# A dynamic depthwise convolution whose taps are three half-precision products instead of one f32 product

## What is computed

```python
def _L1_conv_ref(x, w1, b1, w2, b2):          # x is normalised over channels
    pooled = x.mean(axis=(2, 3))
    h = gelu(pooled @ w1.T + b1)               # exact gelu
    wdyn = (h @ w2.T + b2).reshape(Bs, Cs, 9)  # nine taps for every image and channel
    xp = pad(x, 1, mode='reflect')
    for i in range(3):
        for j in range(3):
            out += xp[:, :, i:i+32, j:j+32] * wdyn[:, :, 3*i+j, None, None]
```

## Time and profile before

| | us |
|---|---|
| median of three runs | 2282.22 |
| lowest, highest | 2279.48, 2284.02 |
| the profiled execution's span | 2530.8 |
| TensorE busy in that span | 1850.5 |
| VectorE busy | 1499.0 |
| ScalarE busy | 1020.8 |
| GpSimd busy | 1003.1 |

### The profile page before, as it was taken

The page is one execution under the profiler, slowest core; times in us unless marked ns, Lnnn a source line. Parts: engine busy times, 40 slices in busy tenths (PEclk is TensorE's granted clock), DMA queues, the critical chain, the costliest instruction groups (busy, mean ns, idle before and its releaser), DMA issues.

```text
span 2530.8 us, 39768 instructions
## 1 busy us (share of the span) xinstructions
PE 1850.5 (73%) x8630; PEld 970.6 (38%) x8631; DVE 1499.0 (59%) x5297; ACT 1020.8 (40%) x1718; POOL 1003.1 (40%) x1180
## 2 busy tenths in 40 slices
PE   0487776777767754999999994988888856888823
PEld 0343332333333322444444442554554433444412
DVE  2766554555545543777677773555555545777768
ACT  0433232332323322666666663434333323555411
POOL 0002344333443343665565564133333323665510
PEclk9788888788887876999999997988888867999955
DMA  9200101001010013222222222111111003222134
GB/s 269 78 17 26 35 33 34 27 26 34 32 34 28 18 39 79 70 67 68 69 65 69 67 69 59 56 51 50 50 51 50 16 16 87 67 68 65 46 116 149
DMA packets 180056, 148.97 MB, mean 59 GB/s; under 512 B 19302, under 2 KB 161822, under 8 KB 179960
## 3 DMA queue, kind: packets, MB, share of 16 engines
q1 hardware_dynamic: 153336, 98.05, 13.8%
q0 software_dynamic: 26624, 49.93, 5.6%
HBM read 76.00 MB, written 77.34 MB: 61 GB/s over the span
## 4 chain that ended last, share of the span: by engine, by line
PE 29%; issue 26%; DVE 16%; another core or an unknown queue 12%; ACT 7%; SPq 5%; DMA 3%; POOL 2%; ACTq 1%; DVEq 0%; POOLq 0%
PE banks L892 7%; PE banks L694 5%; PE banks L695 5%; PE banks L696 5%; PE banks L689 3%; ACT work L980 3%; PE banks L707 3%; SPq L478 2%; SPq L407 1%; DVE small L1282 1%; DMA work<-slot_rows 1%; SPq L479 1%; POOL ffn_rows L609 1%; DVE small L1167 1%
## 5 line engine op out<-in xcount | busy, mean ns | idle before, releaser
L609 POOL DMA_INDIRECT ffn_rows<-work x448 | 469.4, 1048 | 354.2 <-issue 201.8
L588 POOL DMA_INDIRECT slot_rows<-work,small x384 | 387.2, 1008 | 543.8 <-DVE small L1454 422.1
L689 PE MATMUL banks<-small,work 128*128 128x128 f32 x1920 | 301.2, 295 | 276.5 <-ACT work L980 87.9
L689 PEld LDWEIGHTS banks<-small,work 128*128 128x128 f32 x1920 | 242.5, 152 | 385.1 <-issue 187.5
L892 PE MATMUL banks<-work 128*128 128x512 f32 x576 | 301.3, 671 | 0.9 <-DVE work L1716 0.9
L694 PE MATMUL banks<-work,wb_h 128*128 128x512 f16 x648 | 247.2, 382 | 29.9 <-issue 17.7
L1660 DVE TENSOR_TENSOR work<-work 128x512 f16<-128x512 f32 x376 | 259.0, 689 | 12.6
L695 PE MATMUL banks<-work,wb_h 128*128 128x512 f16 x648 | 245.8, 379 | 0.0
L696 PE MATMUL banks<-work,wb_l 128*128 128x512 f16 x648 | 245.8, 379 | 0.0
L694 PE MATMUL banks<-work,wa_h 128*128 128x512 f16 x576 | 241.0, 418 | 3.5 <-ACT work L1011 3.2
L695 PE MATMUL banks<-work,wa_h 128*128 128x512 f16 x576 | 241.4, 419 | 0.0
(11 more groups left out here) (243 smaller groups left out, 2987.7 us busy)
## 6 DMA issues: line engine op xcount, KB each, us to landing
work<-slot_rows SPq DMA_DIRECT2D x112, 264.0 KB
work<-ffn_rows SPq DMA_DIRECT2D x48, 512.0 KB, 4.2
ffn_rows<-small SPq DMA_DIRECT2D x32, 256.0 KB, 3.8
work<-in_x SPq DMA_DIRECT2D x16, 512.0 KB, 3.3
out_image<-work SPq DMA_DIRECT2D x16, 512.0 KB, 2.6
ffn_rows<-work POOLq DMA_INDIRECT x448
slot_rows<-work,small POOLq DMA_INDIRECT x384
slot_rows<-small SPq DMA_DIRECT2D x17, 264.0 KB, 4.0
```

The lines of the kernel that those rows point to most:

```text
L588: pool_e.indirect_dma_start(slots, bass.IndirectOffsetOnAxis(ap=slot_i[:, row_buffer(p, i, k), tt:tt + 1], axis=0), rows[row_buffer(p, i, ...
L609: pool_e.indirect_dma_start(dst, bass.IndirectOffsetOnAxis(ap=idg[old.v][:, qq, 0:1].bitcast(I32), axis=0), yt[old.u][:, qq, :], None, bou ...
L689: last = pe.transpose(dst[:, tt * P:(tt + 1) * P], x, ident)
```

## The change

The tap values and the image are each split into a high and a low part in half precision (f16). A tap is then high x high, high x low and low x high: three f16 matmuls for each half, summed in PSUM. `vpad` has two planes, its inside is filled with the high part by ScalarE, and VectorE subtracts it from the f32 value in PSUM for the low part (semaphore `C_low`), for which GpSimd's border copies and the transposes of the rows now wait instead of `C_inside`. The border copies take both planes at once. On VectorE `split_taps` scales the nine values by a power of two (largest magnitude, exponent bits, its inverse) and splits them in six instructions; the diagonals take both parts in one instruction per third, of 768 elements in f16 instead of 384 in f32. ScalarE's copy of the result to `cacc` multiplies by the power of two. Before the first image one copy makes an f16 identity.

```diff
@@ scratch
-        wd = t([TAPS])
+        wd = t([TAPS + 1])
+        wd_exp, wd_down = t([1]), t([1])
+        wd_up = t([2, 1])
+        wd_hl = t([2, TAPS], F16)
-        vpad = [tC([HP, WP]) for _ in range(2)]
-        diag = tC([TAPS, P])
+        vpad = [tC([2, HP, WP], F16) for _ in range(2)]
+        diag = tC([2, TAPS, P], F16)
+        ident16 = tC([P], F16)
@@ GpSimd, c_step
-                    pool_e.wait_ge(sem("C_inside"), nxt.b + 1)
+                    pool_e.wait_ge(sem("C_low"), nxt.b + 1)
-                    pool_e.tensor_copy(v[:, 0:1, 1:W + 1], v[:, 2:3, 1:W + 1]).then_inc(sem("C_border_done"), 1)
+                    pool_e.tensor_copy(v[:, :, 0, 1:W + 1], v[:, :, 2, 1:W + 1]).then_inc(sem("C_border_done"), 1)
...
@@ TensorE, tap
-                for half in range(2):
-                    h0 = half * (H // 2)
-                    last = pe.matmul(pair[i.u][:, half * 512:(half + 1) * 512], diag[:, k, :],
-                                     vpad[i.u][:, h0 + dy:h0 + dy + H // 2, dx:dx + W],
-                                     start=(k == 0), stop=(k == TAPS - 1))
+                for w, v in ((0, 0), (0, 1), (1, 0)):
+                    for half in range(2):
+                        h0 = half * (H // 2)
+                        last = pe.matmul(pair[i.u][:, half * 512:(half + 1) * 512], diag[:, w, k, :],
+                                         vpad[i.u][:, v, h0 + dy:h0 + dy + H // 2, dx:dx + W],
+                                         start=(k == 0 and w + v == 0), stop=(k == TAPS - 1 and w == 1))
@@ TensorE, c_step
-                    pe.wait_ge(sem("C_inside"), upto(old.b + 3, IMAGES))
+                    pe.wait_ge(sem("C_low"), upto(old.b + 3, IMAGES))
                     route_turn("C_", old)
@@ ScalarE, c_step
-                    act.activation(vpad[nxt.u][:, 1:H + 1, 1:W + 1], tp.rearrange("p (h w) -> p h w", h=H), ACT.Copy,
+                    act.activation(vpad[nxt.u][:, 0, 1:H + 1, 1:W + 1], tp.rearrange("p (h w) -> p h w", h=H), ACT.Copy,
-                    act.activation(cacc, pair[i.u], ACT.Copy).then_inc(sem("C_conv_copied"), 1)
+                    act.activation(cacc, pair[i.u], ACT.Copy, scale=wd_up[:, i.u, :]).then_inc(sem("C_conv_copied"), 1)
@@ VectorE
+            def split_taps(i):
+                ...
+                dve.tensor_reduce(wd_exp, wd, AX_X, ALU.max, apply_absolute_value=True).then_inc(sem("dve_steps"), 1)
+                step()
+                dve.tensor_scalar(wd_exp.bitcast(I32), wd_exp.bitcast(I32), 0x7F800000, None, ALU.bitwise_and).then_inc(sem("dve_steps"), 1)
+                step()
+                dve.tensor_scalar(down.bitcast(I32), wd_exp.bitcast(I32), -1.0, float(0x7E800000), ALU.mult, ALU.add).then_inc(sem("dve_steps"), 1)
+                step()
+                if some(i.b - 1):
+                    dve.wait_ge(sem("C_conv_copied"), i.b - 1)
+                dve.tensor_scalar(up, wd_exp, 2.0, None, ALU.mult).then_inc(sem("C_up"), 1)
+                dve.tensor_scalar(wd_hl[:, 0, :], wd[:, 0:TAPS], down, None, ALU.mult).then_inc(sem("dve_steps"), 1)
+                step()
+                dve.scalar_tensor_tensor(out=wd_hl[:, 1, :], in0=wd[:, 0:TAPS], scalar=down, in1=wd_hl[:, 0, :],
+                                         op0=ALU.mult, op1=ALU.subtract).then_inc(sem("dve_steps"), 1)
+                step()
@@ VectorE, diagonals
-                dve.tensor_tensor(diag[:, k, :], ident.unsqueeze(1).to_broadcast([P, 3, P]), bcast(wd[:, k], P), ALU.mult).then_inc(sem("C_diag"), 1)
+                eye = ident16.unsqueeze(1).unsqueeze(1).to_broadcast([P, 2, 3, P])
+                dve.tensor_tensor(diag[:, :, k, :], eye, wd_hl[:, :, k].unsqueeze(3).to_broadcast([P, 2, 3, P]), ALU.mult).then_inc(sem("C_diag"), 1)
@@ VectorE, c_step
                 if has_nxt:
+                    dve.wait_ge(sem("C_inside"), nxt.b + 1)
+                    v = vpad[nxt.u][:, :, 1:H + 1, 1:W + 1]
+                    dve.tensor_tensor(v[:, 1], tp.rearrange("p (h w) -> p h w", h=H), v[:, 0], ALU.subtract).then_inc(sem("C_low"), 1)
                     dve.wait_ge(sem("C_wd_done"), nxt.b + 1)
-                    dve.tensor_tensor(wd, sm_a[:, 8:8 + TAPS], b2_taps, ALU.add).then_inc(sem("C_wd_read"), 1)
+                    dve.tensor_tensor(wd[:, 0:TAPS], sm_a[:, 8:8 + TAPS], b2_taps, ALU.add).then_inc(sem("C_wd_read"), 1)
                     dve.wait_ge(sem("C_wd_read"), nxt.b + 1)
+                    split_taps(nxt)
                     diagonals(nxt, 0)
                     diagonals(nxt, 1)
```

17 lines of the change are left out of this document (12 added, 5 removed).

## The result

The changed kernel takes 2301.05 us (median of 4, 2300.46 to 2305.31), the kernel before 2283.12 in the same runs: ratio 1.0083, 95% interval 1.0069 to 1.0097. It is 18 us slower. The forecast was 2277, faster. Measured again later beside 19 runs of the kernel before: 2305.14 against 2285.71, ratio 1.0086, interval 1.0069 to 1.0102.

What follows compares the result with a forecast made beforehand. It took a stage C loop through three engines as the bound, no engine being full. The new loop saved 0.89 us in about 14 images (-12.5), the slower clock cost 7: -5.5 from 2282.2 gives 2277, range 2260 to 2296.

Steps and rivals of the forecast that it cites:

- TensorE's products: Stage C taps: three f16 products replace two f32 passes; first part of the loop falls by 2.69 to 11.11 us.
- The loop before, with ScalarE's path as the last: Stage C loop of 24.87 us per image through TensorE and ScalarE, VectorE's parallel path only 0.32 us shorter.
- The splitting (1.2) and the diagonals (+0.82): VectorE's path after the tap values: six splitting instructions add 1.2 us, two longer thirds of diagonals 0.82.
- the second rival: VectorE's diagonals run at twice the rate, 0.47 us a third: 11.5 us further, 2266; chance 0.09.
- The new loop: Stage C: first part 11.11 us plus VectorE's 12.87 gives 23.98 per image, 0.89 less, about -12.5 us over 14 images.
- The section on GpSimd: Stage C borders ready at 18.9 us after the positions; TensorE waits 2.7 us before tap 0, at no cost.
- The first images: First two images of stage C, without routing work: TensorE's gain against VectorE's added 2 us, left at nothing.
- The clock (+7): TensorE's taps 1 to 3 after idle spells: every third image loses 1.55 us more, 7 us in all.
- Rival 1: Longer TensorE idle spells cost taps 1 to 3 the full clock in each image: 2291 to 2295; chance 0.26.
- Rival 5: TensorE's f16 products stay at the f32 spacing of 0.43 us, 8 us more an image: 2340; chance 0.03.
- The unnamed waits: Waits for "remote" in the first profile, 120.6 us in stage C, taken for a product of profiling and left out.
- Rival 3: The unnamed waits belong to every execution, GpSimd's scatters set stage C's loop, change worth nothing: 2282; chance 0.08.

Runs made afterwards that it cites:

- after_warm: Changed kernel with fillers, ten unused f16 products per image on TensorE ahead of the position matmuls in stage C: 2294.74 us, ratio 1.0049 to the kernel before.
- before_again: Kernel before, unchanged, profiled a second time: one run of 2291.64 us, loop 26.59 us per image.
- before_dve_work: Kernel before plus the change's VectorE work (low part, splitting, 768-element diagonals, in f32), keeping its old f32 products: 2324.36 us, ratio 1.0170.
- before_pad: Kernel before with 13 semaphore increments more per image on VectorE in stage C, computing nothing, matching the changed loop's instruction count: 2291.14 us, ratio 1.0021.
- after_again: Changed kernel, unaltered, measured again beside 19 runs of the kernel before: 2305.14 us, ratio 1.0086.
- after_small_add: Changed kernel with GpSimd's addition of expert rows in stage C cut from 1024 elements to 8: 2280.86 us, ratio 0.9981 to the kernel before.
- after_lean_reorder_b: Changed kernel with short splitting (four VectorE steps fewer) and GpSimd's new order (one scatter, borders, row addition, seven scatters): 2280.38 us, ratio 0.9973 to the kernel before.
- after_no_split: Changed kernel without the six splitting instructions, the taps' parts being constants: 2291.34 us, ratio 1.0031 to the kernel before.
- after_reorder_b: Changed kernel with only GpSimd's order in stage C altered (one scatter, borders, row addition, seven scatters): 2289.12 us, ratio 1.0018 to the kernel before.
- before_reorder: Kernel before with GpSimd's order in stage C altered (one scatter, borders, row addition, seven scatters), on a chip with before at 2536.05: 2486.45 us, ratio 0.9798.

## Why the prediction was wrong, point by point

*TensorE's products.* Right. Three f16 products for two f32 passes take the first stretch from 15.09 to 12.86 us. With fillers, nearly at full clock, it is 11.37 (`after_warm`), against 11.11 forecast, and 14.01 in the kernel before: 2.64 less, against 2.69 forecast.

*The loop before, with ScalarE's path as the last and VectorE's 0.32 us behind.* Wrong by little. In `before_again` VectorE starts the choice 0.31 + 0.98 + 6.81 = 8.10 us after the tap addition and the exponential follows 0.82 later, at 8.92, while ScalarE's copy starts at 6.26 and with 1.03 and the table load's 1.28 is through at 8.57. So VectorE's path was the last already, because its small steps lose 0.6 us to the hold in the kernel before too; with the shortened addition the start of the choice moves to 7.57 and the forecast's order holds. On VectorE's path the forecast's own terms give -2.69 + 1.2 + 0.82 + 0.1 = -0.57 per image instead of -0.89: with the 7 us for the clock that is -1 us in 14 images, a forecast of 2281 and no change. The images that the sum was read from the earlier trace rows were one early and one later one.

*The splitting (1.2) and the diagonals (+0.82).* Right: +1.23 and +0.76. 768 elements take 0.95 us in f16 in the changed kernel and 0.95 in f32 in `before_dve_work`. That answers the second rival as well: no double rate with a value repeated along the row. Two thirds in f32 (`before_dve_work`):

```profile
1766.67 1.83 DVE L1746 TENSOR_TENSOR wa_l<-small 128x768 f32<-128x768 f32 x2
```

The two in f16 above took 1.82. The tier table of the Trainium skill ("VectorE: DVE Perf Modes", "The perf-mode tier table (the rule you actually need)") taken alone would have given half; its section on the mode's step of one, "Mode 2×_1P — pack two bf16 into one 32-bit read", agrees with the trace.

*The low part (hidden).* Right: 1.23 us, inside VectorE's wait for the tap values, which still lasts 3.56.

*The new loop, "1627.12 - 1618.95 = 8.17 us".* This is the step that failed. It carried VectorE's chain from the tap values to the choice over unchanged and added the splitting and the diagonals to it. In the kernel before, GpSimd's addition lies for the most part beside statistics, which it doesn't hold; in the changed kernel it lies beside the small steps, which it holds until it ends. Cost: 1.64 us per image, 19.0 us in the twelve images with the full loop. Without it the measured loop would be 0.15 us shorter than before, 2 us in all, where the mended sum of the point above gives 1. The section on GpSimd in the prediction had the pieces: it put the end of the border copies, behind which the next addition stands, 0.7 us later (18.9 instead of 18.2). Measured it is 2.5 later (21.4 instead of 18.9), of which 1.4 come from the longer code, which the sum didn't hold (`before_pad`), 0.4 from the last third of the diagonals, as forecast, and most of the rest from slower scatters (eight take 10.8 us instead of 10.2). But the section priced only TensorE's wait for the borders, which came seven times for 13.6 us in all (below), where 2.7 in each image were forecast; that GpSimd's next instruction lies on VectorE's chain was not asked.

```profile
PE banks L897 <- POOL work L655: 13.6, 7, 3.4
```

*The first images, "left at nothing".* A second term that failed. The prediction saw that VectorE's added 2 us "stand on its next wait" there and left them out. In the profiled pair they cost 9.2 us, and as much with GpSimd's new order; in other profiles of the changed kernel 8.1 (`after_again`) and 6.0 (`after_small_add`). With less added work on VectorE it is less: 5.1 with the short splitting (`after_lean_reorder_b`), 2.8 without any (`after_no_split`). No experiment separates the wait from the half clock that goes with it. The sum also took 14 full images; there are twelve.

*The clock (+7).* The size was right on the loop: the half clock costs the first stretch 1.08 us in the kernel before (15.09 less 14.01 with fillers) and 1.49 in the changed one, 0.4 more, against 0.5 forecast. How it comes about was read wrongly: in the kernel before, seven of the ten images already have a slow first stretch (15.2 to 16.5 us against 13.8), in the changed one nine (12.5 to 13.8 against 11.3), so the size is in part luck. Rival 1 put the whole loss there and would have come near the time (2291 to 2295) for a reason that isn't the main one.

*The code.* Not in the sum. By the packets (97 instead of 71) and the waits, VectorE's longer loop has instructions loaded anew in each pass. Alone it costs 0.2% (`before_pad`), nearly all of it through the hold: it delays GpSimd's addition, and the stretch with the small steps grows from 6.81 to 7.43.

*Two sums.* The end of -20 us (split at 1.0, no further loss by the clock) doesn't follow from its terms: 14 x (0.89 + 0.2) is 15. Rival 5's 2340 is too low, since 5 us in 14 images are 70 and VectorE's added 2.1 stand behind them. Neither changes the outcome.

*The unnamed waits.* The choice was right for these runs and its reason most likely wrong. On two of the chips used here the kernel before takes 2523 to 2542 us in all 16 runs, and profiles from them show such waits. The first profile, with its span of 2530.8, fits them, though on which chip it was taken isn't known. Rival 3 said that they belong to every execution; by the times they belong to every execution on such a chip.

## What to carry to other kernels

When a change shifts a chain of small VectorE steps, lay GpSimd's elementwise operations over the new timeline: one of 2.3 us can hold a step of 0.17 until it ends, and its place in GpSimd's order decides whether it meets steps that it holds or steps that it doesn't. Price the images in which the pipeline fills apart from the full loop: here they were a second loss that the loop didn't show. Before an engine's saving is counted, check over many images, not one, that its path is the last; and count the instructions that a change adds to a loop body, not only their time. Moving GpSimd's addition into VectorE's wait made the original kernel 0.36% faster and needs none of the change.

## What the runs showed of the hardware that was not expected

A GpSimd addition of 128x1024 f32 (2.34 us) held scalar and two-input VectorE steps on eight elements until it ended, and left the statistics steps at their length. A step can be held for longer than the addition lasts, 2.86 us, when it starts beside the border copies that stand ahead of it. Other operations of GpSimd hold a step too: with the addition shortened, the step at L1249 ended with a scatter after 0.22 to 0.43 us in six images and with the last border copy after 0.70 in one (`after_small_add`). VectorE and GpSimd in the changed kernel:

```profile
1670.01 2.86 DVE L1299 TENSOR_SCALAR small<-small 128x8 f32<-128x8 f32 x1
```
```profile
1670.22 0.54 POOL L655 COPY work<-work 128x68 f16<-128x68 f16 x1
1670.51 2.34 POOL L636 TENSOR_TENSOR work<-work 128x1024 f32<-128x1024 f32 x1
```

The other way round, GpSimd's indirect scatters, 0.98 us each elsewhere, took 1.63 and 1.70 us beside VectorE's diagonals and token addition in `after_reorder_b`:

```profile
1598.88 1.63 POOL L592 DMA_INDIRECT slot_rows<-work,small  x1 [0.30 <-issue]
1600.82 1.70 POOL L592 DMA_INDIRECT slot_rows<-work,small  x1 [0.31 <-issue]
1602.82 0.98 POOL L592 DMA_INDIRECT slot_rows<-work,small  x1 [0.30 <-issue]
```

Instruction packets rose from 71 to 97 with 13 added instructions per image in VectorE's program, and stayed at 71 with 20 instructions more in all (5317); in the stage's loop an instruction of VectorE waited 2.1 to 2.7 us once a pass of two images.

Chips differ. Three of the five chips that the experiments ran on took 2283 to 2286 us for the kernel before and two 2536 to 2539. On the latter ScalarE and VectorE wait for something that the trace can't name. Waits over the whole of `before_reorder`:

```profile
ACT small L1038 <- remote: 131.3, 13, 13.0
ACT work L1034 <- remote: 64.0, 10, 9.2
```

GpSimd's new order was worth 2.0% there and 0.36% elsewhere; the loop fell from 31.37 us (the first profile) to 27.18. What these waits are stays open, as does what the change by itself does on such a chip; the changed kernel as it is wasn't run there. With the short splitting and GpSimd's old order it took 2500.55 us where the kernel before took 2536.05, 1.5% less: there such a change may pay by itself. With the new order in both, the changed kernel and the kernel before are equal there (2490.37 and 2486.45 us).
